# Writing out the middle two batches of the attention loop in a fused attention and expert kernel

## What is computed

```
xn = _layernorm(x, axis=-1)
x = x + _L0_attn_ref(xn, w_qkv, w_out) + _L0_ffn_ref(xn, wg, w1, b1, w2, b2)

scores = jnp.einsum('bhnqd,bhnkd->bhnqk', qb, k_kv) * scale
scores = jnp.where(_band_mask(nb), scores, NEG_INF)
attn = jax.nn.softmax(scores, axis=-1)
ob = jnp.einsum('bhnqk,bhnkd->bhnqd', attn, v_kv)
```

## Time and profile before

| | |
|---|---|
| median of 3 runs | 795.09 us (789.34 to 796.57) |
| profiled execution, its time | 789.64 us |
| its span | 788.1 us |
| PE busy, share of the span | 89% |
| DVE / ACT / POOL busy | 64% / 61% / 58% |
| mean granted TensorE clock | 0.947 |
| attention phase | from about 481 us to the end |

### The profile page before, as it was taken

The page is one execution under the profiler, slowest core; times in us unless marked ns, Lnnn a source line. Parts: engine busy times, 40 slices in busy tenths (PEclk is TensorE's granted clock), DMA queues, the critical chain, the costliest instruction groups (busy, mean ns, idle before and its releaser), DMA issues. The chain is left out here.

```text
span 788.1 us, 19233 instructions
## 1 busy us (share of the span) xinstructions
PE 698.7 (89%) x5804; PEld 600.5 (76%) x5805; DVE 506.3 (64%) x1888; ACT 479.3 (61%) x1503; POOL 454.6 (58%) x826
## 2 busy tenths in 40 slices
PE   2644289999999999999999998999999899999884
PEld 2333268989899898989989897788787678788763
DVE  7699335253443425344353524899999879999995
ACT  2442156291744719265380823898989778989972
POOL 2554645151443615335251503899999879999993
PEclk9957679999999999999999997899999989999998
DMA  8460313222142312314222013131323223331311
GB/s 280 149 240 0 126 32 121 75 93 73 67 133 80 104 55 77 116 73 126 87 83 70 8 34 108 29 87 57 116 81 86 93 73 86 86 109 35 109 55 49
DMA packets 50941, 70.12 MB, mean 89 GB/s; under 512 B 4784, under 2 KB 43440, under 8 KB 50864
## 3 DMA queue, kind: packets, MB, share of 16 engines
q1 hardware_dynamic: 44368, 52.37, 20.4%
q0 software_dynamic: 6144, 16.79, 7.4%
q10 hardware_dynamic: 352, 0.04, 0.0%
HBM read 48.28 MB, written 16.78 MB: 83 GB/s over the span
## 5 line engine op out<-in xcount | busy, mean ns | idle before, releaser
L1025 ACT ACTIVATE a_p<-a_p,a_nmax 128x128 f32<-128x128 f32 x512 | 198.3, 391 | 35.5 <-DVE a_nmax L1055 34.9
L956 POOL TENSOR_SCALAR a_p<-a_p,a_rsum 128x128 f32<-128x128 f32 x512 | 198.7, 405 | 21.6 <-DVE a_rsum L1062 19.0
L696 DVE TENSOR_TENSOR m_hl<-m_hf,m_hh 128x512 fp32r<-128x512 f32 x128 | 93.1, 727 | 99.0 <-ACT m_hh L653 99.0
L55 PE MATMUL m_psY<-m_w2h,m_hh 128*128 128x256 f32 x512 | 145.0, 283 | 0.0
L55 PE MATMUL m_psY<-m_w2l,m_hh 128*128 128x256 f32 x512 | 143.9, 281 | 0.0
L55 PE MATMUL m_psY<-m_w2h,m_hl 128*128 128x256 f32 x512 | 143.8, 281 | 0.0
L649 ACT ACTIVATE m_hf<-m_psF,b1T 128x512 f32<-128x512 f32 x128 | 88.3, 690 | 65.2 <-PE m_psF L55 51.1
L617 POOL CAST m_w2h<-raw 128x256 fp32r<-128x256 f32 x64 | 25.5, 399 | 177.4 <-PE m_psY L55 120.5
L1055 DVE CUSTOM_DVE_ANT_0 a_p<-a_psS,mask 128x128 f32<-128x128 f32 x512 | 116.5, 280 | 9.2 <-PE a_psS L1176 4.9
L55 PE MATMUL m_psF<-m_xh,w1h 128*128 128x512 f32 x256 | 103.1, 403 | 1.5 <-DVE m_xl L673 1.5
L55 PE MATMUL m_psF<-m_xh,w1l 128*128 128x512 f32 x256 | 101.6, 397 | 0.0
(11 more groups left out here) (187 smaller groups left out, 1405.1 us busy)
## 6 DMA issues: line engine op xcount, KB each, us to landing
raw<-in_L_ffn_w SPq DMA_DIRECT2D x16, 1024.0 KB, 5.3
y_scratch<-y SPq DMA_DIRECT2D x64, 128.0 KB, 1.7
n_xin<-in_L_attn_x SPq DMA_DIRECT2D x8, 512.0 KB, 7.8
xn_scratch<-n_xn SPq DMA_DIRECT2D x8, 512.0 KB, 2.9
xnr<-xn_scratch SPq DMA_DIRECT2D x8, 512.0 KB, 4.2
a_res<-in_L_attn_x SPq DMA_DIRECT2D x8, 512.0 KB
out<-a_res SPq DMA_DIRECT2D x8, 512.0 KB
b2b<-in_L_ffn_b SPq DMA_DIRECT2D x8, 128.0 KB, 7.4
```

Of the source, the lines that this page charges most:

```text
L55: last = pe.matmul(out, a, b, start=(n_start and i == 0), stop=(n_stop and i == n - 1))
L696: dve.tensor_tensor(hl[:, u // HC, u % HC, :], hf[:, u % FR, :], hh[:, u // HC, u % HC, :].bitcast(fp32), ALU.subtract).then_inc(hl_done, 1)
L956: pool.tensor_scalar(e, e, rsum[:, r, j:j + 1], 0.0, ALU.mult, ALU.add).then_inc(norm_done, 1)
L1025: act.activation(e, e, ACT.Exp, scale=-1.0, bias=nmax[:, r, j:j + 1], accum_out=sums[:, r, j:j + 1]).then_inc(exp_done, 1)
```

## The change

The loop of the middle two batches in `batches` becomes a Python `for`. Every engine's stream then holds the body twice, with b as a constant. The work, its order on each engine and its waits stay as they are.

```
         def batches(eng, body, tail):
 
             body(0, True, False)
-            with eng.Fori(1, B - 1) as b:
+            for b in range(1, B - 1):
                 body(b, False, False)
             body(B - 1, False, True)
             tail(B - 1)
```

## The result

The written-out kernel takes 785.94 us (779.91 to 787.99) against 794.24 before it in the same session. The ratio is 0.9904, with a 95% interval of 0.9885 to 0.9923; on two other chips it was 0.9895 and 0.9885. The predicted 788.0 and its range held. The gain is 8.0 to 8.8 us by the medians of the three sessions, where the sum gave 7.1: direction and mechanism were right, one term was too small. Of the 2.1 us between 788.0 and 785.94, 0.85 is that the median before is 794.24 over twenty runs and was 795.09 over the three that the forecast started from.

What follows compares the result with a forecast made beforehand. In attention PE and DVE are both busy, DVE being the bound; stops of both can't be caught up. Branch back 6.85 plus register rows 0.25 gave 7.1 us, off the median 795.09: 788.0 us, range 781.0 to 790.5.

Steps and rivals of the forecast that it cites:

- The gap belongs to the branch back: Crossing from batch 1 to batch 2: 8.28 us against 1.66 at the other two crossings, blamed on reloading the loop's top.
- 41.80 - 35.17 + 0.22 = 6.85: Attention's middle batches: unit with the branch back less its like without it, plus the longer unit behind; 6.85 us saved.
- The 0.22: Unit behind the branch back: 35.58 us against 35.36 in batch 1, from the lag and the lowered clock.
- The second copy at nothing: Batch 2 written out: loading its new text costs nothing, being covered by the engines' work; 6.85 us if that fails once.
- no stop of issue over 1 us before 730 us: Sign in the changed kernel's trace: PE, DVE and ACT never stop over 1 us for "issue" before 730 us.
- Register rows, 0.25: Rows for waits that compare with a number made from b, in the loop's passes: mostly hidden; 0.25 us gained, between 0 and 0.6.
- The 0.19 us at L1088: DVE's L1088 in each u = 0 unit: 0.69 us in the loop, 0.50 in batch 3; at most 0.19 to gain.
- SP's transfers at nothing: SP's transfers get constant addresses at the same places: nothing to gain or lose.
- The stop stays: Rival at the crossing: something else causes the gap, so straight code stops too; no gain, or 791 to 795 in part; chance 0.12.
- slower: Rival in the second copy, likeliest on PE: code comes late, 6.85 us per late block, 802 us at two; chance 0.04.
- More than the trace shows: Rival: slower runs are slower because the reload takes longer in them; median 782.5 us, a gain of 1.6%; chance 0.12.
- The chances: Whole kernel: 0.36 for faster by over 1% (7.95 us), 0.61 for within 1%, 0.03 for slower by over 1%.

Runs made afterwards that it cites:

- The loop with a hint: The kernel before, its loop kept, with a hint on every engine that the branch will go back to the top; ratio 0.9933, repeated 0.9948 (789.26 us).
- the one-pass kernel: The kernel before with two loops of one pass each in place of the loop of two passes; ratio 0.9864, repeated 0.9882 (785.14 us).

## Why the prediction was right, and where it was off

- *The gap belongs to the branch back.* Right, and now shown, but more narrowly: it belongs to what the branch back leads to. The loop with a hint takes the branch, keeps its register rows and has no stop; the kernels in which one engine loops have that engine's stop and that engine's extra packets.
- *41.80 - 35.17 + 0.22 = 6.85.* The first part held in the second profile (41.74 - 35.31 = 6.43). The 0.22 was the term that was too small. It is the tail of the lowered clock, and was 0.2 us in one execution and 1.8 (37.00 - 35.19) in the other. With the mean of the two profiles, 7.5, and the register rows at nothing, the sum would have been 7.5 against 8.0 to 8.8 measured. The rest, about 1 us, isn't placed; the work ahead of the attention, the same in all kernels but for the experts' loop, scatters by more than that (first L1136 at 480.6 to 484.0 us on these chips). I took one execution's aftermath for the price of the stop; the earlier trace rows showed a clock of 0.96 in the unit behind, which was the sign that its length would vary.
- *The second copy at nothing.* Right: no stop of "issue" over 0.4 us in batches 1 and 2, and the written-out experts' loop agrees. The queues moved 32 and 36 packets instead of 35 and 42, so about as many, as foretold. One sign failed by its letter: "no stop of issue over 1 us before 730 us" is broken by DVE's 1.68 us at 514.55, ahead of the changed text.
- *Register rows, 0.25.* Not told from nothing. Only the hinted kernel keeps them on all engines without the stop. Its four middle units sum to 141.30 us, those of the written-out kernel to 140.91 on the same chip, and to 140.75 and 141.19 in its two other profiles. On the first chip the hinted kernel's take 143.99 and those of the one-pass kernel 142.50, but there its unit of batch 0, which has no such rows, is longer by 0.3 as well (35.66 against 35.35). The 0.19 us at L1088 isn't the register's: at the step of batch 3 that took 0.50 before, the written-out kernel has

```profile
725.50 0.69 DVE L1088 SCALAR_TENSOR_TENSOR a_res<-a_yg,gates,a_res 128x256 f32<-128x256 f32 x1
```

- *SP's transfers at nothing.* Nothing in the traces speaks against it.
- *The rivals.* "The stop stays" and "slower" didn't come. "More than the trace shows" came in a weak form: the branch back does cost more in some executions, by the clock behind it and not by a longer reload.
- *The chances.* The ratio's interval lies on both sides of the 1% that I set as the bound, as the forecast just below it implied.
- *Small slips.* POOL's 6.9 us of waiting for DVE are not all the wake of PE's second gap: 2.1 of them follow DVE's own stop. DVE's digits in the experts go from 2 to 5 and not from 3. The range's lower end, 782.2 less 0.35, is 781.9; the 781.0 isn't worked out. None of this moves the forecast.
- *The 5.45 us between the profiled run and the median.* Taking the sum off the median was right: the medians moved by 8.3, and the spread stayed (8.8 us before and 8.1 written out, over twenty runs each).

## What to carry to other kernels

The loops of this case were free where the top was at hand when the engine went back: look at the queues of instructions in the stretch of the loop, and if packets flow in every pass, compare the work across the branch back with the same work at the entry and at the exit. Writing such a loop out cost nothing here, as the straight code was loaded under the work, and the short loop of the experts gained nothing by it. The stop that idled TensorE also took the granted clock down, to 0.74 in the crossing and to 0.91 or 0.96 in the unit behind it, so price such a stop as a range from more than one profile. And count the instructions of a control kernel before relying on what it keeps: the one-pass loops had lost the rows that they were to hold, which shows in their number, 18463 and not some 19200, and in no time.

## What the runs showed that was not expected

Much of the scatter between executions goes with the granted clock. The first unit of batch 0 took 38.71 us in one written-out execution and 36.13 in another kernel whose attention is the same text (the second with both loops written out):

```profile
480.74:519.45 38.71, 36.47 (x339) 29.48 (x337) 31.17 (x184) 32.17 (x147) 30.68 (x69) 0.78 0.21 65
```

```profile
480.62:516.75 36.13, 32.48 (x339) 26.53 (x337) 31.23 (x186) 32.27 (x149) 29.70 (x69) 0.91 0.22 69
```

The granted clock is 0.78 in the one and 0.91 in the other. DVE's stop in batch 0, 1.55 us in the first of them, isn't the reason: the kernel before took 38.50 us at 0.78 without it. Between 504 and 515 us the clock was 0.69 in the written-out kernel's first profile and 1.00 in the second profile of before. 2.6 us here and up to 4 in the last stretch are a good part of the 8 us that were being measured; both came in kernels with and without the loop.
